# Propagation rounds of a graph network: rings of five groups instead of four, and layers and rounds written out

## The reference

```python
def prop(z):
    return segment_sum(edge_weight[:, None] * z[src], dst, num_segments=N_SUP)

for i in range(5):                       # layers
    z = h @ W[i] + b[i]
    x_start = prop(z)
    xi = h
    for _ in range(5):                   # rounds
        xi = (prop(xi) + x_start) / 2.9
    out = gamma[i] * (xi - mean(xi, 0)) / sqrt(var(xi, 0) + 1e-5) + beta[i]
    h = where(out > 0, out, 0.01 * out)
return h[seg_ids]                        # seg_ids is zero everywhere here
```

## Time and profile before

| | |
|---|---|
| median of 3 runs | 12018.62 us |
| lowest, highest | 12002.51, 12023.15 us |
| profiled execution | 11995.85 us |
| its span | 11994.1 us |
| granted TensorE clock, mean over the span | 0.687 |
| PE busy (x33931 instructions) | 6782.4 us (57%) |
| DVE busy (x20811) | 6277.9 us (52%) |
| POOL busy (x6508) | 6513.3 us (54%) |
| ACT busy (x3027) | 1432.6 us (12%) |
| DMA queues for instructions | 51 and 116 packets, 0.0% |

### The profile page before, as it was taken

How to read it: one execution, slowest core, us unless ns; L and a number is a source line. 1 busy time by engine, 2 the same in 40 slices (tenths; PEclk the granted TensorE clock), 3 DMA queues, 4 the chain that set the end, 5 groups by cost and what they waited for, 6 DMA issues and landing times. The chain is left out here.

```text
span 11994.1 us, 149789 instructions
## 1 busy us (share of the span) xinstructions
PE 6782.4 (57%) x33931; PEld 5074.2 (42%) x33931; DVE 6277.9 (52%) x20811; ACT 1432.6 (12%) x3027; POOL 6513.3 (54%) x6508
## 2 busy tenths in 40 slices
PE   3544547665567656567656667655567266570072
PEld 2333214443356444356443446544346144560051
DVE  5576545555545555545555554555554755550067
ACT  0022003000002000001100000200000500351005
POOL 4667351555643556553455654356554555676646
PEclk8755767766677766667776667776667577785555
DMA  3143001344422344421334431334431511692106
GB/s 121 38 159 122 2 2 54 70 82 83 84 47 65 69 79 84 82 56 40 87 76 83 84 63 30 92 73 84 83 72 31 181 48 52 146 200 37 24 20 267
DMA packets 526027, 950.80 MB, mean 79 GB/s; under 512 B 187011, under 2 KB 269788, under 8 KB 525604
## 3 DMA queue, kind: packets, MB, share of 16 engines
q0 software_dynamic: 192000, 330.22, 18.4%
q1 hardware_dynamic: 316196, 516.19, 13.8%
q10 hardware_dynamic: 17664, 102.61, 2.1%
HBM read 502.28 MB, written 458.64 MB: 80 GB/s over the span
## 5 line engine op out<-in xcount | busy, mean ns | idle before, releaser
L965 POOL DMA_INDIRECT G<-tab,gidx x4000 | 3805.8, 951 | 3554.8 <-issue 1897.5
L1401 PE MATMUL PS<-G,M 128*128 128x128 f32 x8000 | 2131.7, 408 | 1945.6 <-DVE G L396 1626.8
L1401 PEld LDWEIGHTS PS<-G,M 128*128 128x128 f32 x8000 | 1722.9, 276 | 2402.2 <-DVE G L396 1827.1
L1386 PE MATMUL PS<-G,lring 128*1 128x128 f32 x8000 | 1498.3, 348 | 224.9 <-DMA G<-tab,gidx 184.4
L398 DVE SCALAR_TENSOR_TENSOR G<-G,whole,PS 1x128 f32<-1x128 f32 (+1 forms) x3300 | 1103.5, 334 | 823.7 <-issue 128.2
L1346 DVE TENSOR_TENSOR Y<-PS,big 128x512 f32<-128x512 f32 x800 | 553.4, 692 | 1334.0 <-remote 1079.2
L419 DVE TENSOR_SCALAR M<-keyrow,keycol,wccol 128x128 f32 (+1 forms) x4004 | 1135.3, 364 | 29.3 <-issue 8.2
L1386 PEld LDWEIGHTS PS<-G,lring 128*1 128x1 f32 x8000 | 719.6, 100 | 779.7 <-DMA G<-tab,gidx 226.7
L1355 ACT COPY big<-PS 128x512 f32 x200 | 117.0, 585 | 5453.5 <-remote 3647.8
L1397 PE MATMUL PS<-M,G 128*128 128x128 f32 x1600 | 486.3, 401 | 437.9 <-DVE G L396 431.6
L1066 POOL DMA_INDIRECT Y<-pair_d,G x400 | 402.3, 1006 | 359.7 <-DMA pair_d<-UT 207.4
(11 more groups left out here) (498 smaller groups left out, 11639.0 us busy)
## 6 DMA issues: line engine op xcount, KB each, us to landing
tab<-Y SPq DMA_DIRECT2D x1000, 256.0 KB
big<-agg SPq DMA_DIRECT2D x90, 832.0 KB, 12.7
G<-tab,gidx POOLq DMA_INDIRECT x4000
big<-x SPq DMA_DIRECT2D x60, 832.0 KB, 8.8
xt_d<-big SPq DMA_DIRECT2D x30, 858.0 KB, 13.6
x2n<-big ACTq DMA_DIRECT2D x30, 838.5 KB
big<-x2n SPq DMA_DIRECT2D x30, 838.5 KB
agg<-big ACTq DMA_DIRECT2D x30, 832.0 KB
```

What stands on the lines that cost most here:

```text
L965: pool.indirect_dma_start(G[:, t % RG, 0:D], None, tab_in(k), bass.IndirectOffsetOnAxis(ap=gidx[:, t:t + 1], axis=0)).then_inc(l_got[t % R ...
L1386: nc.tensor.matmul(PS[0:1, CAR, j, :], lring[:, GR * h + j:GR * h + j + 1], G[:, s, 0:D], start=True, stop=True).then_inc(l_row, 1)
L1401: ins = nc.tensor.matmul(PS[:, SUM + h, j, :], M[:, GR * h + j, :], G[:, s, 0:D], start=True, stop=True)
```

## The change

The rings hold five groups: RG=20, NG=5, so that a round is exactly LI=10 turns of the ring and no remainder is left. POOL's waits stand at t=20, 28, ..., 196, and the last asks for 45 groups instead of 46. The layer loop, the group loop and ACT's loop of round k=4 are Python loops now: each engine's program holds all 4 layers and 20 rounds, with constants in every wait and address. Because five is odd, the half (h) that alternates is `(i + q) % 2` of the group instead of `q % 2`. To make room for the larger Y and G, two buffers of the last stage's attention (ALT, FW) are laid into M and Y, and the row buffer `cf` is replaced by a smaller one. In layer 0 the SP loads of coefficient rows use the five slots of Y, while PSUM banks stay four. Cut to its core:

```diff
-RG = 16
+RG = 20
 NG = RG // GR
 LI = T // RG
-LREM = (T - LI * RG) // GR
...
-        def group_loop(eng):
-
-            with eng.Fori(0, LI) as i:
-                for q in range(NG):
-                    yield i, q
-            for q in range(LREM):
-                yield LI, q
+        def group_loop():
+
+            for n in range(T // GR):
+                yield n // NG, n % NG
...
         def l1_gather(pool, l, k):
             g0 = 2 * rounds(l, k)
-            stored = [16 * slot_uses(q) * round_no(l, k + 1) for q in range(NG)]
-            steady(pool, *stored)
+            stored = 16 * LI * round_no(l, k + 1)
+            steady(pool, stored)
             for q in range(NG):
-                pool.wait_ge(l_tab[q], stored[q])
+                pool.wait_ge(l_tab[q], stored)
             for t in range(T):
-                if t >= RG and t % U == 0:
-                    free = g0 + (t - RG) // GR + 2
+                if t >= RG and (t - RG) % U == 0:
+                    free = g0 + min((t - RG) // GR + 2, (T - RG) // GR)
                     steady(pool, free, OPS * free + 1)
                     pool.wait_ge(l_sum, free)
                     pool.wait_ge(l_ch, OPS * free + 1)
...
         def half(i, q):
 
-            return NG // 2 * i + q // 2
+            return (NG * i + q) // 2
...
         def l1_dve(dve, l, k):
             g0 = 2 * rounds(l, k)
             last = k == NL - 1
-            for i, q in group_loop(dve):
-                h, g, tile = q % 2, g0 + NG * i + q, RG * i + GR * q
+            for i, q in group_loop():
+                h, g, tile = (i + q) % 2, g0 + NG * i + q, RG * i + GR * q
                 dve.wait_ge(l_sum, g)
...
-                    dve.wait_ge(l_tab[q], 16 * (slot_uses(q) * round_no(l, k + 1) + i))
+                    dve.wait_ge(l_tab[q], 16 * (LI * round_no(l, k + 1) + i))
...
         def last_act(act, l):
-            with act.Fori(0, IT) as i:
+            for i in range(IT):
...
         def over_layers(eng, program):
 
-            program(0)
-            with eng.Fori(1, NL) as l:
+            for l in range(NL):
                 program(l)
...
-        ALT = sb("ALT", [TG, 2, HEADS, P])
-        FW = sb("FW", [TG, 2, HEADS, P])
+        ALT = M[0:TG].rearrange("p (g q) i -> p g q i", g=2)
+        FW = Y[0:TG, 0:U, :].rearrange("p (g q) i -> p g q i", g=2)
```

More of the change, by code:

```diff
@@ L36, in build @@
 def build(nc, x0, src, dst, ea, ew, w0, b0, w1, b1, gamma, beta, w2, b2, we, be, coef, linw, linb, asrc, adst, out):
-    assert CHUNKS % SLOTS == 0 and T * TE == E and IT * U == T and LI * RG + LREM * GR == T and NG % 2 == 0 and LREM % 2 == 0 and CHUNKS * NJ == NC_ and CHUNKS % 2 == 0
+    assert CHUNKS % SLOTS == 0 and T * TE == E and IT * U == T and LI * RG == T and T // GR % 2 == 0 and CHUNKS * NJ == NC_ and CHUNKS % 2 == 0
     ctx = ExitStack()
@@ L981, in two_ahead @@
                 one(0, q)
-            for i, q in group_loop(eng):
-                if not (isinstance(i, int) and i == LI):
+            for i, q in group_loop():
+                if NG * i + q + 2 < T // GR:
                     one(i + (q + 2) // NG, (q + 2) % NG)
@@ L1255, in scalars_act @@
                 act.wait_ge(o_ex, g + 1)
-                nc.scalar.copy(zt_of(g // NG, g % NG), PS[:, g % NG, :, :]).then_inc(l_xc, 1)
+                nc.scalar.copy(zt_of(g // NG, g % NG), PS[:, g % 4, :, :]).then_inc(l_xc, 1)
         def turn_act(act, l):
@@ L1262, in scaled @@
             def scaled(i, q):
-                h, f = q % 2, IT * (l - 1) + half(i, q)
+                h, f = (i + q) % 2, IT * (l - 1) + half(i, q)
                 steady(act, f)
@@ L1293, in turn_pe @@
         def turn_pe(pe, l):
-            for i, q in group_loop(pe):
-                h = q % 2
+            for i, q in group_loop():
+                h = (i + q) % 2
                 pe.wait_ge(l_hc[h], 2 * IT * (l - 1) + half(i, q) + 1)
@@ L1302, in inner_act @@
         def inner_act(act, l):
-            for i, q in group_loop(act):
-                h, n = q % 2, IT * (l - 1) + NG // 2 * i + q // 2
+            for i, q in group_loop():
+                h, n = (i + q) % 2, IT * (l - 1) + half(i, q)
                 steady(act, IT * l, n)
@@ L1311, in got_before @@
         def got_before(l, k, slot):
-            return (LI + (1 if slot < GR * LREM else 0)) * (NL * (l - 1) + k)
+            return LI * (NL * (l - 1) + k)
         def inner(l, k):
@@ L1328, in l1_dve @@
                 if inner(l, k):
-                    n = IT * (l - 1) + NG // 2 * i + q // 2
+                    n = IT * (l - 1) + half(i, q)
                     dve.wait_ge(l_z[h], n + 1)
@@ L1368, in l1_pe @@
             last = k == NL - 1
-            for i, q in group_loop(pe):
-                h, g, tile = q % 2, g0 + NG * i + q, RG * i + GR * q
+            for i, q in group_loop():
+                h, g, tile = (i + q) % 2, g0 + NG * i + q, RG * i + GR * q
                 gl = 2 * IT * l + NG * i + q
                 if inner(l, k):
-                    n = NG // 2 * i + q // 2
+                    n = half(i, q)
                     pe.wait_ge(l_hc[h], 2 * IT * (l - 1) + IT + n + 1)
@@ L1461, in layer @@
                         bl = b1[bass.ds(l, 1), :].rearrange("a f -> (a f)")
-                    if not isinstance(l, int):
+                    if l:
                         sp.wait_ge(l_ev, 2 * rounds(l, 0) + 1)
@@ L1477, in layer @@
                 def layer(l):
-                    if isinstance(l, int):
+                    if l == 0:
                         scalars_pool(pool)
```

26 lines of the change are left out of this document (11 added, 15 removed).

## The result

The changed kernel takes 12117.44 us (median of 4 runs, 12106.35 to 12121.2), the kernel before, in the runs beside them, 12020.89 us: a ratio of 1.008 with a 95% interval of 1.0062 to 1.0097. The forecast was 11967, that is faster; the measured time is slower, and lies inside rival C's 12070 to 12172.

The account below looks back on a forecast made before the run. POOL's wait for room in the ring, released by late-seen PE signals, was taken as the bound. Terms -37-14-14-6+20 = -51 us on 11995.85 gave 11945, plus 22.8 to the median: 11967 us, range 11410 to 12125.

Parts of the forecast that it names:

- rival C: Merged runs of gathers at each round's start and end cost 5.1 to 10.2 us a round: 12070 to 12172; chance 0.23.
- The bound: POOL waits for a place in the ring; a PE signal fired late in a gather run is seen only after it.
- In k=1 to 3 it only lengthens the idle before a held signal: nothing: Written-out code saves DVE 0.83 us a group, but in these rounds DVE is not on the path: 0 us.
- the 23 pairs of a round: Steady part: one more group of slack does not bring the odd group's sum earlier; 10.05+2.0 us per pair still, gain 0.
- k=0: First round of each layer: written-out code saves 0.4 us in each of 23 pairs, over 4 layers -37 us.
- k=4 and the turn: Written-out code saves 0.15 us in each of 23 pairs of k=4 (-14 us), and -6 us in the turns.
- Start and end: Round edges: deeper ring moves the first wait later and the last earlier; +4.0 or -6.0 us a round, taken as 0.
- The loops' turns: Loop turns in the rounds cost 0.21 us, before a wait with 3 us to spare; removing them gains nothing.
- the longer programs: PE and DVE load 9,038 and 7,982 more rows of code: +20 us, bounds 0 and +82.
- The rest: Registers and branches gone from SP, POOL and ACT, stored-row waits five groups back, layer 0 and attention parts: nothing.
- The rival of dear turns: Each of 12 loop turns a round costs DVE or PE 1.92 us; removal gives -461 us, 11506; chance 0.05.
- Rival B: POOL's gap in k=1 to 3 is a ring one group too short; the fifth group swallows it: about 11425; chance 0.25.

Follow-up runs that it names:

- loops5: The changed kernel (ring of five, POOL 20 ahead, layers written out) with rounds and turns as loops again; 1.0016 (0.9996 to 1.0037) of the kernel before.
- ahead16: The changed kernel, code still written out, with the old waits, so POOL is again only 16 gathers ahead; 1.0034 (1.0006 to 1.0063) of the kernel before.

## Why the prediction was wrong

- *The bound.* Right: POOL's wait for room, released by a signal of PE that is seen late. The reading of the held signal is right for the runs of 8 and too simple beyond them. It is not held in every run: in the steady pairs above, what was fired up to 6.7 us into the run was let through, what was fired at 7.5 was held, and k=2 of `loops5` puts the edge between 7.16 and 7.34. In the first run of a round a sum fired at 9.8 us was let through. And in long runs signals come through before the run is over. The earlier trace rows could have warned: behind 16 gathers DVE started 2.6 us after the last one's end, behind 8 it was 1.6, where the prediction has "the same 2 us".
- *The step that failed* is "In k=1 to 3 it only lengthens the idle before a held signal: nothing", with the 23 pairs of a round costed at nothing. The faster groups (3.86 to 3.88 us instead of 4.36) bring the awaited sum 0.8 us earlier into the run, 6.7 instead of 7.5 us, and so to the other side of that edge. Instead of 0 this came to +33 us a round, as the mean of all 12.
- *Rival C* had the mechanism (a merged run costs more than two) and, for the sum, nearly the right time, but for the wrong place: it put one or two merged runs at a round's edges, 5.1 us each. In fact each of some ten merged runs a round costs 27.3-24.1=3.2 us. That its time came out is luck as far as the place goes. `ahead16`, which has no run of 20, shows that the edges are not needed for it.
- *k=0* was forecast at -9 us a round and gave -49; *k=4 and the turn* at -5 and gave -23. The sign was right, the terms were mis-sized: 49 us over 23 pairs is 2.1 us each where 0.4 was taken, and 23 us with the turn is at most 1.0 where 0.15 was. `ahead16` and `loops5` show that the written-out rounds bring both. That a signal which comes earlier escapes being held there too is my guess, not shown. These gains are why the loss is 97 us and not 12x33, some 390.
- *Start and end.* The start was forecast with the second sum held until 1.6 us after the run, 26.4 us in. It was seen at 18.7, so the first wait did not stop POOL. The run of 28 gathers that follows and the pause of 8.77 us behind it belong to the merging, so the 0 taken for start and end was never tested by itself.
- *The loops' turns* and *the longer programs*: the instruction queues went from 167 to 422 packets. I found no stall that I could put down to them, and the +20 has no row that tests it. The rival of dear turns falls for k=1 to 3, which lost with the loops gone; in k=0 and k=4 no run parts the turns from the rest of the code.
- *The rest* was taken at nothing; 30 of the 125 us between the two profiled executions lie outside the four layers. What they are is open.
- *Rival B* falls: `loops5` has the fifth group and keeps gaps of 2.5 us or more in most pairs.

Nothing is settled on what in the chip holds the signals. Shown is that long runs of indirect gathers on POOL go with it, that landing data do not make it, that 15 us of plain DMAs on POOL do not either, and that a pause in the right place ends it.

## What to carry to other kernels

Where one engine's signal is seen late only while another is issuing, the time at which it is fired against that engine's run matters more than the speed of either. Making the waiting side faster can tip a cycle into a worse one, so look at the new period in the timeline rather than at busy times. A deliberate pause of the engine that everything waits for, halfway between its real waits, took the written-out kernels 4.4 and 5.5% under the kernel before, which neither the deeper ring nor the written-out code did alone. It needs its place and its code: at the real waits it gave 1.6 to 1.7%, and in the looped kernel, at the real waits, it lost 0.7%.

## What was not expected of the hardware

- Sums that PE fires late in a run of indirect gathers are seen 1.6 us after the end of a run of 8 and 2.7 us after one of 16. The local sums fired about 7.7 us into a run of 16 were seen at 14.8 us, 5.0 us before its end. Signals of DVE reach PE in the same stretch without delay (PE's L1392 at 2814.04 follows DVE's L397 of 2813.65).
- A plain DMA of 128 rows of 512 B occupies POOL for 0.54 us, an indirect one for 0.95 us with 0.30 us in front. A sum fired 13.7 us into a run of plain DMAs was seen in 0.04 us.
- With the gathers out of the way the rounds went at 3.60 us a group, and PE's granted clock stood at 0.97 in that stretch, nearly always the upper of its two levels (2.4 GHz), against 0.67 in the changed kernel's k=1, where PE was busy for less than half of the time.
